# Layer 0's running maximum, over pairs of chunks as b + relu(a - b), with the row maximum inside one VectorE instruction

## The chip, the cores and the metric

One core of one Trainium2 chip runs the whole program. The metric is device microseconds from start to end; lower is better. The engines are TensorE (PE, with weight loads listed as PEld), VectorE (DVE), ScalarE (ACT), GpSimd (POOL) and SyncE (SP), which issues the DMAs.

## The reference

Two perceiver layers on x (1 x 128 x 256). The change touches the first block of layer 0, a cross attention of 128 queries over 12544 keys, 16 heads of 16 channels:

```python
q = (query @ Wq + bq).reshape(B, Nq, H, D).transpose(0, 2, 1, 3)
k = (key_value @ Wk + bk).reshape(B, Nkv, H, D).transpose(0, 2, 1, 3)
v = (key_value @ Wv + bv).reshape(B, Nkv, H, D).transpose(0, 2, 1, 3)
attn = jnp.einsum('bhqd,bhkd->bhqk', q, k) * scale
attn = jax.nn.softmax(attn, axis=-1)
x = jnp.einsum('bhqk,bhkd->bqhd', attn, v).reshape(B, Nq, Cq)
```

The rest (a gated linear attention, two feed-forward blocks, a masked cross attention with 64-channel heads, a self attention with distance bias) is the same in both kernels.

## The kernel before

The softmax of layer 0's cross attention takes two passes over the keys. A first pass (the maximum pass) finds each query's and head's largest score in a coarse product. A second pass (the sum pass) computes the exponentials and weighs the values. Both go by chunks of 896 keys (`CH`), 14 of them (`NCH`); a chunk's columns are two halves of 448 (`NB`).

In the maximum pass SP loads a chunk's context into `raw`. ACT rounds it into `ct` (`split_max0`, two casts). PE projects it to keys in four blocks (`project_max0`, two matmuls each, PSUM banks 4 and 5) and ACT adds the bias and stores each block in `kn` (`key_block_max0`). For each of 16 heads PE multiplies the head's queries with the two halves of the keys into a pair of PSUM banks (`heads_max0`). Three pairs of banks take turns (`HEAD_BANKS`), so a head's matmuls wait until the head three places before it has been read. Even heads are read by DVE, which reduces the 896 scores to one (`reduce_head`, line 813). Odd heads are read by ACT, which casts them to bf16 into one of two `stage` buffers (line 555), and DVE takes an elementwise maximum of that into `acc`, which holds one row of 896 running maxima for each odd head (`accumulate_head`, line 819). After the last chunk DVE halves `acc` three times and reduces it (lines 878 and 880). `merge_max0` (line 823) folds the even heads' maxima into `mx`.

No order is written down beyond program order on each engine; semaphores do the rest. PE's queue has, for each chunk, heads 0 to 2, a block of the next chunk's projection, heads 3 to 5, a block, and so on. ACT has besides, in the first chunks, seven counts of the mask (`mask_sum`), and ahead of chunk 12 two sums over the feed-forward weights (line 580), which SP loads once the seventh count is done. The last chunk's maximum pass is interleaved with the first chunk's exact projection (`project0`, five matmuls of 448 columns) and values (`values0`, five of 256), whose results are read by ACT and DVE (`key_block_hi`, `key_block_lo`, the copies on line 870). At the start POOL fills `acc` (line 390) and part of `ks` (line 398), and takes the power that the first layer norm needs between those two (line 385).

## Time and profile before

| | |
|---|---|
| time, median of 3 runs | 1162.57 us (1161.85 to 1162.88) |
| profiled execution, its own time | 1163.62 us |
| its span, first to last instruction | 1161.8 us |
| maximum pass, first head matmul to last merge | 28.1 to 243.7 us of the span |
| ACT's first read of a head | 30.4 us of the span |
| PE busy in the span | 958.8 us (83%) |
| DVE busy in the span | 645.5 us (56%) |
| ACT busy in the span | 539.8 us (46%) |

The span is shorter than the execution's own time by what lies around the first and last instruction. Busy shares over the whole span average stages with different limits; the maximum pass is some 215 us of them. "Granted clock" is the share of full speed at which TensorE was allowed to run.

### The profile page before, as it was taken

To read this page: it belongs to the slowest core of one execution; us is meant where nothing else is said; L and a number is where in the kernel's file an instruction comes from. 1 tells how busy PE (TensorE), PEld (TensorE's weight loads), DVE (VectorE), ACT (ScalarE), POOL (GpSimd) and SP (SyncE) were. 2 spreads that over 40 slices of the span, in tenths; PEclk is the share of its full clock that TensorE was granted. 3 is DMA by queue.
4 is the path that set the end of the run, shared out by engine and by line. 5 is a ranking of instruction groups with operands and counts; after the bars stand their busy time and mean duration, and the time that the engine had idled before them with its cause. 6 is when DMAs were issued, how large, how long until landed. Compare 5 with 4: busy or idle time off the path is not lost.

```text
span 1161.8 us, 21208 instructions
## 1 busy us (share of the span) xinstructions
PE 958.8 (83%) x7648; PEld 702.1 (60%) x7651; DVE 645.5 (56%) x936; ACT 539.8 (46%) x626; POOL 176.2 (15%) x93
## 2 busy tenths in 40 slices
PE   3877888749899999999969578886999979998514
PEld 2544555537677777777747365555777767776403
DVE  4777999862111222222250237994779757777592
ACT  2787888626666666666646313002333323332011
POOL 4000000141111111111193031242004030000000
PEclk9978999878999999999999689998999989999665
DMA  7213121154556555566614332211001000000000
GB/s 209 82 30 120 48 70 57 33 126 95 129 128 152 131 126 126 134 146 145 144 32 97 109 101 56 64 36 32 1 5 33 1 6 1 1 1 1 1 0 5
DMA packets 37319, 81.73 MB, mean 70 GB/s; under 512 B 9553, under 2 KB 17426, under 8 KB 37138
## 3 DMA queue, kind: packets, MB, share of 16 engines
q1 hardware_dynamic: 37266, 81.01, 28.1%
q8 instruction: 35, 0.57, 0.2%
q14 instruction: 18, 0.15, 0.0%
HBM read 41.54 MB, written 0.13 MB: 36 GB/s over the span
## 4 chain that ended last, share of the span: by engine, by line
PE 46%; issue 19%; DVE 11%; SPq 9%; DMA 7%; ACT 6%; POOL 1%; DVEq 1%; ACTq 0%; POOLq 0%
PE ps L1498 10%; SPq L310 8%; DMA ks<-khl 6%; PE ps L1508 6%; PE ps L1291 5%; PE ps L1519 5%; PE ps L1303 4%; PE ps L1273 4%; PE ps L1245 4%; PE ps L1500 2%; DVE cm L813 2%; ACT pr L555 1%; DVE pr L819 1%; DMA raw<-in_ctxT 1%; PE ps L1282 1%
## 5 line engine op out<-in xcount | busy, mean ns | idle before, releaser
L617 ACT ACTIVATE pr<-ps 128x1024 f32<-128x1024 f32 x196 | 200.0, 1026 | 131.7 <-DVEq L966 127.9
L1291 PE MATMUL ps<-qs,ks 128*128 128x256 f32 x784 | 147.0, 310 | 21.8 <-DMA ks<-khl 13.9
L1245 PE MATMUL ps<-ks 128*128 128x448 f32 x448 | 134.5, 422 | 33.7 <-ACT pr L555 14.3
L1291 PEld LDWEIGHTS ps<-qs,ks 128*128 128x128 f32 x784 | 106.8, 192 | 64.2 <-issue 33.0
L695 ACT ACTIVATE pr<-ps 128x1024 f32<-128x1024 f32 x56 | 57.5, 1027 | 184.7 <-DVE ps L1096 184.7
L1498 PE MATMUL ps<-ks,ct 128*128 128x512 f32 x448 | 128.3, 408 | 7.2 <-issue 4.6
L813 DVE TENSOR_REDUCE cm<-ps 128x1 f32<-128x896 f32 x112 | 120.5, 1084 | 16.9 <-PE ps L1245 16.0
L1245 PEld LDWEIGHTS ps<-ks 128*128 128x128 f32 x448 | 80.7, 206 | 76.8 <-DVE cm L813 28.0
L1303 PE MATMUL ps<-pr,v 128*17 128x128 f32 x3136 | 124.6, 277 | 0.2 <-ACT pr L617 0.2
L847 DVE SCALAR_TENSOR_TENSOR khl<-ps,bk,khl 128x448 fp32r<-128x448 f32 x56 | 38.2, 682 | 151.0 <-ACT khl L592 151.0
L1096 DVE TENSOR_SCALAR ps<-ps 128x1024 f32<-128x1024 f32 x56 | 68.9, 1231 | 76.5 <-PE ps L1500 76.5
L405 POOL TENSOR_TENSOR ct<-raw,ct 128x896 fp32r<-128x896 f32 x14 | 30.6, 2188 | 501.6 <-ACT ct L537 501.6
L910 DVE COPY v<-ps 128x256 f32<-128x256 f32 x91 | 38.6, 424 | 115.1 <-PE ps L1282 115.1
L1498 PEld LDWEIGHTS ps<-ks,ct 128*128 128x128 f32 x448 | 81.2, 190 | 32.1 <-issue 16.6
L1303 PEld LDWEIGHTS ps<-pr,v 128*17 128x17 f32 x3136 | 69.2, 97 | 36.3 <-issue 15.8
L1282 PE MATMUL ps<-wv,ct 128*128 128x256 f32 x490 | 75.1, 283 | 3.2 <-DVE v L870 2.2
L1082 DVE TENSOR_TENSOR nm<-nm,pr 128x1024 f32<-128x1024 f32 x56 | 73.3, 1308 | 2.1
L1273 PE MATMUL ps<-ct,wk 128*128 128x448 f32 x280 | 69.9, 381 | 2.2 <-POOL ct L408 1.6
L1062 DVE CUSTOM_DVE_ANT_0 pr<-ps,khl 128x896 f32<-128x896 f32 x64 | 67.4, 1086 | 4.5 <-issue 4.2
L1078 DVE TENSOR_TENSOR pr<-pr,wraw 128x1024 f32<-128x1024 f32 x56 | 69.1, 1235 | 0.0
L1282 PEld LDWEIGHTS ps<-wv,ct 128*128 128x128 f32 x490 | 65.4, 190 | 5.4 <-DVE v L870 4.3
L1508 PE MATMUL ps<-ks,ct 128*128 128x512 f32 x280 | 68.6, 391 | 0.0
(259 smaller groups left out, 1325.6 us busy)
## 6 DMA issues: line engine op xcount, KB each, us to landing
ks<-khl SPq DMA_DIRECT2D x168, 224.0 KB, 4.8
raw<-in_ctxT SPq DMA_DIRECT2D x36, 448.0 KB, 3.7
raw<-in_ctxT SPq DMA_DIRECT2D x54, 224.0 KB, 4.2
ffw<-in_mask_q SPq DMA_DIRECT2D x1, 1568.0 KB, 10.0
ffw<-in_W1T SPq DMA_DIRECT2D x1, 1024.0 KB, 4.9
ffw<-in_W2T SPq DMA_DIRECT2D x1, 1024.0 KB, 7.2
pr<-in_Wq SPq DMA_DIRECT2D x1, 1024.0 KB, 5.1
pr<-in_Wkt SPq DMA_DIRECT2D x1, 1024.0 KB, 7.4
```

What stands on the lines that cost most here:

```text
L310: sp.dma_start(ks_v[32 * slot:32 * slot + 32, b, g::4, :].bitcast(F32), khl[32 * g:32 * g + 32, part, :, :].bitcast(F32)).then_inc(S[f"e0_ ...
L617: nc.scalar.activation(pr[:, (HALVES * b + u) % 4, :], bank(2 * (u % 2), 2), ACT.Exp).then_inc(S["e0_exp"], 1)
L813: V.tensor_reduce(cm_e[:, h // 2:h // 2 + 1, b], ps[:, bank:bank + 2, 0:NB], AX_XY, ALU.max).then_inc(S["m0_red"], 1)
L1078: V.tensor_tensor(sl, sl, mk[:, b, u // 2, :].unsqueeze(1).to_broadcast([P, 8, T]), ALU.mult).then_inc(S["e1_masked"], 1)
L1082: V.tensor_tensor(acc, acc, pr[:, (HALVES * b + u) % 4, :], ALU.add).then_inc(S["e1_sum"], 1)
L1245: last = mm(ps[:, bank + n, 0:NB], qn[:, h, :], kn[:, b, t, n * NB:(n + 1) * NB], start=True, stop=True)
L1273: last = mm(dst, wk0[:, w, t * P:(t + 1) * P], ct[:, b, xx, n * NB:(n + 1) * NB], start=(j == 0), stop=(j == 4))
L1282: last = mm(ps[:, bank, 0:C], ct[:, b, xx, t * P:(t + 1) * P], wv0[:, w, :], start=(j == 0), stop=(j == 4))
L1291: last = mm(ps[:, 2 * z + k // 2, (k % 2) * 256:(k % 2) * 256 + 256], ks_v[:, b, gg, t * P:(t + 1) * P], qs[:, gg * 256:gg * 256 + 256], s ...
L1303: last = mm(ps[32 * j:32 * j + 17, 4, (h // 4) * T:(h // 4 + 1) * T], v17_v[:, b, t, h, :], pr[:, (HALVES * b + u) % 4, k * T:(k + 1) * T] ...
L1498: mm(ps[:, 2 * z + j, :], xx[:, t * P:(t + 1) * P], asp[:, w, cols], start=(i == 0), stop=False)
L1508: last = mm(ps[:, 6 + j, :], ct[:, b, xx, t * P:(t + 1) * P], wv1[:, w, 512 * j:512 * j + 512], start=(i == 0), stop=(i == 4))
```

## The change

Chunks are taken in pairs, a the second and b the first, so there are seven pairs (`NSUP`). The product with a head's queries is linear in the keys, and max(a, b) = b + relu(a - b). ACT stores the keys of b (`base_keys`, both halves at once); DVE subtracts them from the projected keys of a (`key_differences`). For each head PE makes two products, called units: unit 2h with the key differences, unit 2h + 1 with b's keys. Units take the three pairs of banks in turn. ACT reads unit 2h through relu into one of four fp32 `stage` slots (`above_base`); DVE adds unit 2h + 1 from PSUM to that slot and takes the row maximum in the same instruction (`head_max`, behind a memset of one element). `merge_max0` comes once a pair. `acc` and its halving are gone, and with them POOL's first fill; POOL's second fill is shorter, and the rest of it comes at the start of the last pair. In the first pair ACT's queue has the casts of chunks 2 and 3 ahead of the first relu. A block of the projection is now four matmuls. The second of two `kn` buffers lies in the part of `ks` that is free in this pass.

The diff, without most of the lines that it takes out (they stand in the kernel above):

```diff
+UNITS = 2 * H
+SLOTS = 4
+
+
+def unit_bank(u):
+
+    return HEAD_BANKS[u % 3]
+
+
+def last_user(u):
+
+    if u >= 3:
+        return 0, u - 3
+    return -1, max(v for v in range(UNITS) if v % 3 == u % 3)
...
-        kn = ks[:, k0_at + HQ:].rearrange("p (b t n) -> p b t n", b=2, t=2)
+        kn = [ks[:, k0_at + HQ:].rearrange("p (e t n) -> p e t n", e=2, t=2),
+              ks[:, 0:4 * CH].rearrange("p (e t n) -> p e t n", e=2, t=2)]
...
-        acc = pr_flat[:, 0:4 * CH].bitcast(BF16).rearrange("p (j n) -> p j n", j=8)
-        stage = [oacc_flat[:, 0:CH // 2].bitcast(BF16),
-                 pr_flat[:, 4 * CH:4 * CH + CH // 2].bitcast(BF16)]
+        stage = pr_flat[:, 0:SLOTS * CH].rearrange("p (i k n) -> p i k n", i=SLOTS, k=2)
...
             load_max0(3, False)
-            load_max0(4, False)
-            load_max0(5, False)
+            with sp.Fori(4, 11) as c:
+                load_max0(c, False)
             sp.wait_ge(S["mask_sum"], NSUP)
             load(ffw1, a["W1T"].rearrange("(k p) n -> p k n", k=2), "ld_ffw")
             load(ffw2, a["W2T"].rearrange("(k p) n -> p k n", k=8), "ld_ffw")
 
-            with sp.Fori(6, NCH) as c:
+            with sp.Fori(11, NCH) as c:
                 load_max0(c, False)
...
 
 
-            pool.wait_ge(S["acc_init"], 1)
             pool.wait_ge(S["power"], 1)
-            nc.gpsimd.memset(ks[96:P, 0:k0_at - 8 * T].bitcast(F32), 1.0).then_inc(S["ks_ones"], 1)
+            nc.gpsimd.memset(ks[96:P, 4 * CH:k0_at - 8 * T].bitcast(F32), 1.0).then_inc(S["ks_ones"], 1)
...
             split_lo0(0, 0)
+            pool.wait_ge(S["e0_lo"], 2)
+            pool.wait_ge(S["m0_head"], UNITS * NSUP)
+            nc.gpsimd.memset(ks[96:P, 0:4 * CH].bitcast(F32), 1.0).then_inc(S["ks_ones"], 1)
+            pool.wait_ge(S["ks_ones"], 2)
             split_lo0(1, 1)
...
-                act.wait_ge(S["m0_proj"], 4 * c + 4)
+                act.wait_ge(S["m0_proj"], 2 * c + 2)
...
-            def key_block_max0(c, b, i):
-                t, n = i // 2, i % 2
-                if i == 0:
-                    act.wait_ge(S["m0_head"], H * c + H)
-                act.wait_ge(S["m0_proj"], 4 * c + i + 9)
-                nc.scalar.activation(kn[:, b, t, n * NB:(n + 1) * NB], ps[:, 4 + i % 2, 0:NB], ACT.Identity,
-                                     bias=bk0[:, t:t + 1]).then_inc(S["m0_keys"], 1)
+            def base_keys(s, t):
+
+                if t == 0:
+                    act.wait_ge(S["m0_head"], UNITS * s)
+                act.wait_ge(S["m0_proj"], 4 * s + t + 5)
+                nc.scalar.activation(kn[s % 2][:, 0, t, :].rearrange("p (k n) -> p k n", k=2), ps[:, 4:6, 0:NB],
+                                     ACT.Identity, bias=bk0[:, t:t + 1]).then_inc(S["m0_keys"], 1)
...
+            def above_base(s, h):
+
+                at = unit_bank(2 * h)
+                act.wait_ge(S["m0_head"], UNITS * s + 2 * h + 1 + UNITS)
+                act.wait_ge(S["m0_red"], H * s + h - SLOTS + 1 + H)
+                nc.scalar.activation(stage[:, h % SLOTS], ps[:, at:at + 2, 0:NB], ACT.Relu
+                                     ).then_inc(S["m0_staged"], 1)
+
+            split_max0(0, 0)
+            for t in range(2):
+                base_keys(0, t)
+            split_max0(1, 1)
+            split_max0(2, 0)
+            split_max0(3, 1)
+            for s in range(NSUP - 1):
+                for h in range(H):
+                    above_base(s, h)
+                    if h in (3, 6):
+                        base_keys(s + 1, (3, 6).index(h))
+                    if h == 8:
+                        if s < NSUP - 2:
+                            split_max0(2 * s + 4, 0)
+                        else:
+                            act.wait_ge(S["m0_proj"], 4 * (NSUP - 1) + 6)
                             split_hi0(0, 0)
...
+                    if h == 14 and s < NSUP - 2:
+                        split_max0(2 * s + 5, 1)
+                    if h in (10, 12) and 2 * s + (h - 10) // 2 < NSUP:
+                        mask_sum(2 * s + (h - 10) // 2)
+                if s == 4:
+                    act.wait_ge(S["ld_ffw"], 32)
+                    act.wait_ge(S["mask_sum"], NSUP)
+                    for k in range(2):
+                        nc.scalar.activation(scrap, ffw[:, 2048 * k:2048 * k + 2048], ACT.Abs,
+                                             accum_out=wsum[:, k:k + 1]).then_inc(S["wsum"], 1)
+                        act.wait_ge(S["wsum"], k + 1)
...
-            for j in range(8):
-                act.wait_ge(S["m0_head"], H * (NCH - 1) + 2 * j + 34)
-                act.wait_ge(S["m0_acc"], 8 * (NCH - 1) + j + 1)
-                nc.scalar.copy(stage[j % 2].rearrange("p (k n) -> p k n", k=2), ps[:, 2:4, 0:NB]
-                               ).then_inc(S["m0_staged"], 1)
-                if j < 4:
-                    key_block_hi(0, j, 22 + j + 1, None)
-            act.wait_ge(S["m0_proj"], 4 * NCH + 8)
+            for h in range(H):
+                above_base(NSUP - 1, h)
+                if h in (2, 4, 6, 8):
+                    i = h // 2 - 1
+                    key_block_hi(0, i, 22 + i + 1, None, at=4)
...
+
+            def key_differences(s, t, buf):
+
+                dve.wait_ge(S["m0_head"], UNITS * s)
+                dve.wait_ge(S["m0_keys"], 2 * s + t + 1)
+                dve.wait_ge(S["m0_proj"], 4 * s + t + 7)
+                V.scalar_tensor_tensor(kn[buf][:, 1, t, :].rearrange("p (k n) -> p k n", k=2), ps[:, 4:6, 0:NB],
+                                       bk0[:, t:t + 1],
+                                       kn[buf][:, 0, t, :].rearrange("p (k n) -> p k n", k=2).bitcast(F32),
+                                       ALU.add, ALU.subtract).then_inc(S["m0_diff"], 1)
+
+            def head_max(s, h):
+
+                at = unit_bank(2 * h + 1)
+                dve.wait_ge(S["m0_head"], UNITS * s + 2 * h + 2 + UNITS)
+                dve.wait_ge(S["m0_staged"], H * s + h + 1 + H)
+                V.memset(pause2[:, h % 2:h % 2 + 1], 0.0)
+                nc.vector.tensor_tensor_reduce(
+                    out=stage[:, h % SLOTS], in0=ps[:, at:at + 2, 0:NB], in1=stage[:, h % SLOTS],
+                    scale=1.0, scalar=-3.0e38, op0=ALU.add, op1=ALU.max,
+                    accum_out=cm[:, h:h + 1]).then_inc(S["m0_red"], 1)
+
+            def merge_max0(s):
+
+                dve.wait_ge(S["m0_red"], H * s + 2 * H)
+                V.tensor_tensor(mx[:, :], mx[:, :], cm[:, :], ALU.max).then_inc(S["m0_merge"], 1)
+
+            def pair_max0(s, buf):
+                dve.wait_ge(S["m0_merge"], s + 1)
+                for h in range(H):
+                    head_max(s, h)
+                    if h in (9, 12):
+                        key_differences(s + 1, (9, 12).index(h), 1 - buf)
+                merge_max0(s)
+
+            for t in range(2):
+                key_differences(0, t, 0)
+            pair_max0(0, 0)
+            with dve.Fori(1, NSUP - 2, 2) as s:
+                for e in range(2):
+                    pair_max0(s + e, 1 - e)
+            pair_max0(NSUP - 2, 1)
+
...
-            dve.wait_ge(S["m0_merge"], NCH)
...
-                if h % 2 == 0:
-                    reduce_head(NCH - 1, 1, h, 0)
-                else:
-                    accumulate_head(NCH - 1, h // 2)
-                if h == 2:
-                    merge_max0(NCH - 2, 0)
+                head_max(NSUP - 1, h)
                 if h in (2, 4, 6, 8):
-                    key_block_lo(0, h // 2 - 1)
+                    key_block_lo(0, h // 2 - 1, at=4)
...
-            merge_max0(NCH - 1, 1)
-            dve.wait_ge(S["m0_merge"], NCH + 2)
-            dve.wait_ge(S["m0_acc"], 8 * NCH + 2)
-            n = CH // 2
-            while n >= CH // 8:
-                link(V.tensor_tensor(acc[:, :, 0:n], acc[:, :, 0:n], acc[:, :, n:2 * n], ALU.max))
-                n //= 2
-            link(V.tensor_reduce(mx_e[:, :, 1], acc[:, :, 0:CH // 8], AX_X, ALU.max))
+            merge_max0(NSUP - 1)
+            dve.wait_ge(S["m0_merge"], NSUP + 1)
...
-            def project_max0(c, b, blocks=range(4)):
-                if 0 in blocks:
-                    pe.wait_ge(S["m0_split"], c + 1)
-                for i in blocks:
-                    t, n = i // 2, i % 2
-                    pe.wait_ge(S["m0_keys"], 4 * c + i + 3)
-                    dst = ps[:, 4 + i % 2, 0:NB]
-                    mm(dst, wk0[:, W_AH, t * P:(t + 1) * P], ct[:, b, X_AH, n * NB:(n + 1) * NB],
+            def project_max0(s, e, t):
+
+                if t == 0:
+                    pe.wait_ge(S["m0_split"], 2 * s + e + 1)
+                if (e, t) in ((0, 0), (1, 1)):
+                    pe.wait_ge(S["m0_diff"], 2 * s + t + 2)
+                else:
+                    pe.wait_ge(S["m0_keys"], 2 * s + e + 1)
+                for n in range(2):
+                    dst = ps[:, 4 + n, 0:NB]
+                    mm(dst, wk0[:, W_AH, t * P:(t + 1) * P], ct[:, e, X_AH, n * NB:(n + 1) * NB],
                        start=True, stop=False)
-                    mm(dst, wk0[0:64, W_BH, t * P:(t + 1) * P], ct[0:64, b, X_B, n * NB:(n + 1) * NB],
-                       start=False, stop=True).then_inc(S["m0_proj"], 1)
-
-            def heads_max0(c, b, heads, last_chunk=False):
+                    last = mm(dst, wk0[0:64, W_BH, t * P:(t + 1) * P], ct[0:64, e, X_B, n * NB:(n + 1) * NB],
+                              start=False, stop=True)
+                last.then_inc(S["m0_proj"], 1)
+
+            def heads_max0(s, buf, heads):
                 for h in heads:
                     t = h // 8
                     if h % 8 == 0:
-                        pe.wait_ge(S["m0_keys"], 4 * c + 2 * t + 6)
-
-
-
-                    bank = head_bank(b, h)
-                    back, user = last_user(b, h)
-                    if last_chunk:
-                        bank = 2 * (h % 2)
-                        back, user = (0, h - 2) if h > 1 else (-1, {0: H - 1, 1: H - 3}[h])
-                    pe.wait_ge(S["m0_staged" if user % 2 else "m0_red"],
-                               8 * (c + back) + user // 2 + 1 + 8)
-                    for n in range(2):
-                        last = mm(ps[:, bank + n, 0:NB], qn[:, h, :],
-                                  kn[:, b, t, n * NB:(n + 1) * NB], start=True, stop=True)
-                    last.then_inc(S["m0_head"], 1)
+                        pe.wait_ge(S["m0_keys"], 2 * s + t + 1)
+                        pe.wait_ge(S["m0_diff"], 2 * s + t + 3)
+                    for u, e in ((2 * h, 1), (2 * h + 1, 0)):
+                        back, user = last_user(u)
+                        pe.wait_ge(S["m0_red" if user % 2 else "m0_staged"],
+                                   H * (s + back) + user // 2 + 1 + H)
+                        for n in range(2):
+                            last = mm(ps[:, unit_bank(u) + n, 0:NB], qn[:, h, :],
+                                      kn[buf][:, e, t, n * NB:(n + 1) * NB], start=True, stop=True)
+                        last.then_inc(S["m0_head"], 1)
 
             pe.wait_ge(S["w0_hi"], 1)
             pe.wait_ge(S["qn"], 1)
-            project_max0(0, 0)
-
-            def chunk_max0(c, b):
+            for e in range(2):
+                for t in range(2):
+                    project_max0(0, e, t)
+
+            def pair_max0(s, buf):
 
                 for i in range(4):
-                    heads_max0(c, b, range(3 * i, 3 * i + 3))
...
-            with pe.Fori(0, NCH - 2, 2) as c:
-                for b in range(2):
-                    chunk_max0(c + b, b)
-            chunk_max0(NCH - 2, 0)
-
-            def project0(c, b, i):
+                    heads_max0(s, buf, range(3 * i, 3 * i + 3))
+                    project_max0(s + 1, i // 2, i % 2)
+                heads_max0(s, buf, range(12, H))
+
+            pair_max0(0, 0)
+            with pe.Fori(1, NSUP - 2, 2) as s:
+                for e in range(2):
```

In PE's queue inside a chunk, before: the last head unit of a group of three, the projection block, and the next unit. A row with `m0_red` waits for DVE, one with `m0_staged` for ACT.

```order
L1245 MATMUL ps<-ks 128x448 [waits m0_red]
L1245 MATMUL ps<-ks 128x448
L1222 REGISTER_ALU
L1224 MATMUL ps<-ct,wk 128x448 [waits m0_keys]
L1226 MATMUL ps<-ct,wk 128x448
L1245 MATMUL ps<-ks 128x448 [waits m0_staged]
L1245 MATMUL ps<-ks 128x448
```

The same place in the changed kernel, in its first pair (line 1234 is a unit's matmul, 1217 and 1219 are the projection's):

```order
L1234 MATMUL ps<-ks 128x448 [waits m0_red]
L1234 MATMUL ps<-ks 128x448
L1234 MATMUL ps<-ks 128x448 [waits m0_staged]
L1234 MATMUL ps<-ks 128x448
L1217 MATMUL ps<-ct,wk 128x448 [waits m0_keys]
L1219 MATMUL ps<-ct,wk 128x448
L1217 MATMUL ps<-ct,wk 128x448
L1219 MATMUL ps<-ct,wk 128x448
L1234 MATMUL ps<-ks 128x448 [waits m0_red]
```

The block has become twice as long, it stands behind three heads of two units each, and the unit behind it waits for DVE.

ACT's queue ahead of its first read of a head, before (522 and 523 are a chunk's casts, 530 a key block):

```order
L522 CAST ct<-raw 128x896 [waits m0_proj,m0_raw]
L523 CAST ct<-raw 64x896
L530 ACTIVATE ks<-ps,bk 128x448 [waits m0_proj,m0_head]
L530 ACTIVATE ks<-ps,bk 128x448 [waits m0_proj] x3
L522 CAST ct<-raw 128x896 [waits m0_proj,m0_raw]
L523 CAST ct<-raw 64x896
L555 CAST oacc<-ps 128x896 [waits m0_acc,m0_head]
```

And in the changed kernel (520 and 521 are the casts, 528 the keys of b, 552 the relu):

```order
L520 CAST ct<-raw 128x896 [waits m0_proj,m0_raw]
L521 CAST ct<-raw 64x896
L528 ACTIVATE ks<-ps,bk 128x896 [waits m0_proj,m0_head]
L528 ACTIVATE ks<-ps,bk 128x896 [waits m0_proj]
L520 CAST ct<-raw 128x896 [waits m0_proj,m0_raw]
L521 CAST ct<-raw 64x896
L520 CAST ct<-raw 128x896 [waits m0_proj,m0_raw]
L521 CAST ct<-raw 64x896
L520 CAST ct<-raw 128x896 [waits m0_proj,m0_raw]
L521 CAST ct<-raw 64x896
L552 ACTIVATE pr<-ps 128x896 [waits m0_red,m0_head] x4
```

Four chunks are cast ahead of the first relu, where two were cast ahead of the first read.

## Rows read from the trace of the kernel before

**Rows 1.** Busy time of each engine in one steady chunk, granted clock behind POOL.

```profile
163.07:175.67 12.60, 11.11 (x42) 6.56 (x40) 12.50 (x19) 10.61 (x15) 0.00 (x0) 1.00 0.18 55
```

**Rows 2.** Timeline of a steady stretch, PE's weight loads: start, length, both in us.

```profile
117.18 0.19 PEld L1224 LDWEIGHTS ps<-ct,wk 128*128 128x128 f32 x1
...
118.07 0.71 PEld L1245 LDWEIGHTS ps<-ks 128*128 128x128 f32 x4 [0.21 <-issue]
```

**Rows 3.** Timeline, from a unit's first weight load to its reader on ACT.

```profile
212.20 0.70 PEld L1245 LDWEIGHTS ps<-ks 128*128 128x128 f32 x4 [0.21 <-issue]
...
212.91 0.91 ACT L555 CAST oacc<-ps 128x896 bf16<-128x896 f32 x1 [0.15 <-PE ps L1245]
```

**Rows 4.** Timeline, ACT at work without a wait.

```profile
118.77 0.96 ACT L522 CAST ct<-raw 128x896 fp32r<-128x896 f32 x1
...
120.45 0.90 ACT L555 CAST pr<-ps 128x896 bf16<-128x896 f32 x1
121.25 0.64 ACT L530 ACTIVATE ks<-ps,bk 128x448 fp32r<-128x448 f32 x1
...
121.78 0.90 ACT L555 CAST oacc<-ps 128x896 bf16<-128x896 f32 x1
```

**Rows 5.** Timeline of layer 1's maximum pass: an add with row maximum, and PE behind it.

```profile
713.17 1.09 DVE L1062 CUSTOM_DVE_ANT_0 pr<-ps,khl 128x896 f32<-128x896 f32 x1
...
714.32 0.19 PEld L1476 LDWEIGHTS ps<-ct,ks 128*128 128x128 f32 x1 [0.32 <-DVE cm L1062]
```

**Rows 6.** Groups by line: the fused bias and subtraction, columns count, busy, mean ns.

```profile
L847 DVE SCALAR_TENSOR_TENSOR khl<-ps,bk,khl 128x448 fp32r<-128x448 f32 x56 | 38.2, 682 | 151.0 <-ACT khl L592 151.0
```

**Rows 7.** Timeline of the start: POOL, DVE, ACT, PE and SP's queue (SPq).

```profile
1.04 6.07 POOL L390 MEMSET pr<- 128x7168 bf16 x1
...
3.52 0.15 DVE L755 TENSOR_SCALAR rstd<-mv 128x1 f32<-128x1 f32 x1
...
7.74 6.73 DVE L758 TENSOR_SCALAR xn<-x,mv,rstd 128x256 f32<-128x256 f32 x1 [4.07 <-POOL rstd L385]
7.83 6.49 POOL L398 MEMSET ks<- 32x7680 f32 x1
...
9.29 0.40 ACT L514 CAST wv<-wraw 128x256 fp32r<-128x256 f32 x1
...
15.37 0.37 ACT L505 COPY xnT<-ps 128x256 f32<-128x256 f32 x1 [5.67 <-PE ps L1196]
...
19.51 0.98 SPq L240 DMA_DIRECT2D raw<-in_ctxT  x2
...
22.76 0.71 PE L1224 MATMUL ps<-ct,wk 128*128 128x448 f32 x1 [3.15 <-issue]
...
24.07 0.74 PE L1224 MATMUL ps<-ct,wk 128*128 128x448 f32 x1
...
24.73 7.81 SPq L281 DMA_DIRECT2D qs<-ks  x12
...
37.41 0.94 ACT L522 CAST ct<-raw 128x896 fp32r<-128x896 f32 x1 [1.89 <-DMA raw<-in_ctxT]
```

**Rows 8.** Timeline around the weights' loads and the sums over them.

```profile
94.27 0.39 SPq L240 DMA_DIRECT2D ffw<-in_W1T  x1
...
104.49 0.94 ACT L522 CAST ct<-raw 128x896 fp32r<-128x896 f32 x1 [3.38 <-DMA raw<-in_ctxT]
...
204.10 1.91 ACT L580 ACTIVATE v<-ffw 128x2048 bf16<-128x2048 f32 x1
...
206.13 0.91 ACT L555 CAST oacc<-ps 128x896 bf16<-128x896 f32 x1
```

**Rows 9.** Timeline of the last chunk and what follows it.

```profile
237.17 0.65 PEld L1282 LDWEIGHTS ps<-wv,ct 128*128 128x128 f32 x5 [1.06 <-DVE v L870]
...
243.73 7.31 DVE L878 TENSOR_TENSOR pr<-pr 128x3584 bf16<-128x3584 bf16 x3
...
252.20 0.17 DVE L891 TENSOR_SCALAR mx<-mx 128x16 f32<-128x16 f32 x1
```

122 lines of the change are left out of this document (26 added, 96 removed).

## The prediction

> **What bounds the kernel now.** I read the page first (PE 83% busy, no engine full), then the maximum pass stretch by stretch, then single hand-overs in the timeline. In a steady chunk of 12.60 us DVE is busy for 12.50, PE for 11.11 and ACT for 10.61, at granted clock 1.00 [rows 1]. The reader is to see that DVE alone sets the pace: eight reductions, eight adds of staged maxima and a merge. Two chunks cost 25.2 us. After the last merge three halvings and a reduction of the running maxima hold everything up, from 243.73 to the next step at 252.20 [rows 9]. The pass starts late because DVE's layer-norm step takes 6.73 us while POOL fills `ks` for 6.49, and POOL's power ahead of it stood behind another fill of 6.07 [rows 7].
>
> **The work of a pair, by counts.** ACT: 16 relus of 896 columns 0.80 apart (120.45 to 121.25), four casts at 1.68 for a chunk's two (118.77 to 120.45), two key stores that take 0.53 at 448 columns and by the columns about 0.9 at 896 [rows 4]: 18.0 us. DVE: 16 add-and-maximum instructions at most 1.15 apart [rows 5], two key differences (0.68 at 448 columns [rows 6], so about 1.1), a merge: 21 us. PE: a projection part of two matmuls takes 0.89 (117.18 to 118.07), so a block of four 1.78, four blocks 7.1; a unit takes about 0.4 (four loads in 0.71, matmuls behind them) [rows 2], 32 units 12.8: 20 us. By counts a pair would fall from 25.2 to 21.
>
> **What the order makes of it.** Unit 2h goes into the banks that unit 2h - 3 used, which DVE read for head h - 2. So there is a loop: DVE done with head h - 2, PE makes unit 2h, ACT takes its relu, DVE adds head h. Before, ACT's read gave its banks back without DVE. The links: from a unit's first load to its reader 0.71 (212.20 to 212.91) [rows 3]; the relu 0.91, as the cast of the same columns, and 0.04 to hand over; from the start of DVE's instruction to PE's next load 1.15 (713.17 to 714.32; layer 1's pass has the same memset and instruction) [rows 5]. Together 2.81 for two heads, 22.5 a pair if nothing stands in the way.
>
> But each engine takes its queue in order, and the loop has no room to catch up. I walked one pair through at full clock: L is the first load of unit 2h, A the relu's start, D DVE's. L(h) is the latest of D(h-2) + 1.15 and PE being free; unit 2h + 1 goes 0.4 later, but not before A(h-1) is over; A(h) is L + 0.71 or ACT free; D(h) is A + 0.95 or DVE free. A block of 1.78 stands on PE behind h = 2, 5, 8, 11; key stores on ACT behind 3 and 6, casts behind 8 and 14; differences on DVE behind 9 and 12.
>
> | h | L | A | D |
> |---|---|---|---|
> | 0 | 0 | 0.71 | 1.66 |
> | 1 | 1.40 | 2.11 | 3.06 |
> | 2 | 2.81 | 3.52 | 4.46 |
> | 3 | 5.40 | 6.11 | 7.06 |
> | 4 | 6.20 | 7.76 | 8.71 |
> | 6 | 10.90 | 11.61 | 12.56 |
> | 9 | 16.40 | 17.11 | 18.06 |
> | 10 | 17.20 | 17.91 | 20.14 |
> | 12 | 22.10 | 22.81 | 23.76 |
> | 15 | 26.99 | 28.10 | 29.05 |
>
> Each block takes PE for 1.78 where the loop leaves it 0.6 a head, and delays L by 1.2 to 1.5 (5.40 where 4.21 was due); the parity of the delayed head changes, so nothing is won back. The next pair's first two units wait for ACT's and DVE's last head (`last_user` wraps to units 30 and 31): its second unit goes at 30.2, and its h = 3 at 34.64. So a pair takes 34.64 - 5.40 = **29.2 us**, 4.0 more than now. Bounds: 22.5 if blocks cost nothing, 29.2 plus some for the clock (below).
>
> **Start.** The fill of `acc` is gone, so the power can follow DVE's step of 3.52 at once and the layer norm is released near 4.3. POOL's remaining fill is 4096 of 7680 columns, 6.49 x 0.53 = 3.46, and DVE gets through with it near 7.9 instead of 14.5. ACT, however, casts weights until 9.69 (9.29 + 0.40), so its copy of 15.37 comes at 9.7: 5.7 us earlier [rows 7]. PE's first projection moves from 22.76 to 17.1.
>
> That is lost again. Chunk 1 is loaded from 19.51, which SP's queue of small loads sets, and with the 4.9 us that chunk 2 needed (32.54, the end of the 12 DMAs, to 37.41) it lands at 24.4 or a little later. ACT casts it (1.68), until 26.5. SP's 12 DMAs for the queries now run from 20.5 to 28.3 (7.81), chunk 2's load follows and lands at 33.2, its cast ends at 35.0, chunk 3's load needs that cast, lands at 39.8, and is cast until 41.5. Only then comes the first relu, where ACT's first read was at 30.4 (table of the profile before); the loads' times are from [rows 7]. In the walk A(0) is 0.71, so the pair starts at 40.8. PE has waited and runs at half clock at first (two matmuls 1.31 apart, 22.76 to 24.07 [rows 7], a block 2.62): h = 3 stands at 47.6 instead of 46.2, 1.4 more. Start of the pair: 42.2.
>
> Here the Trainium skill's page "SBUF — State Buffer", section "Who interferes with whom", is weighed: a DVE instruction in a two-port mode and a GpSimd one block each other for a whole instruction, whoever issues first. In this trace DVE was released at 7.74, before POOL's 7.83, and still took 6.73 [rows 7]. By the row the layer norm ends near 7.9, by the rule with DVE first some 3 us sooner. The sum is the same, since ACT's weight casts end at 9.69 either way.
>
> **The rest of the pass.** Six pairs: 6 x 29.2 = 175.2. Seven mask counts, two a pair: each holds ACT some 1.8 (2.03 for 2048 columns [rows 8], here 1792), most of it in ACT's gaps; in the walk a pair with two ends 0.6 later: 2.1. Weights: SP loads them after the seventh count and chunk 11 behind them; from 94.27 to 104.49 that took 10.2 [rows 8]. The count now ends at 20.6 of pair 3, chunk 11 lands at 30.9, and its cast is due at 26.4: 4.5. The sums over the weights hold ACT 4.1 (2 x 2.03) where 0.9 of it was idle: 3.1. After these two holds PE is at half clock for some us: 1 each, 2 (0 to 4). Last pair: same walk with five-matmul projections behind h = 1, 3, 5, 7 and values behind 8 to 14. It goes like the others until 13.0; then the first values wait for DVE's last key block (16.4), and each further head costs PE two units, five value matmuls (0.65 [rows 9]) and a wait for DVE's copy of the values two before, 1.2 to 2.4. D(15) starts at 30.0 and the merge ends at 31.3.
>
> Sum: 42.2 + 175.2 + 2.1 + 4.5 + 3.1 + 2 + 31.3 = 260.4, where the next step now starts at 252.20 [rows 9], and there is no halving. 8.2 us later. Behind it nothing is new: keys are stacked by DMA meanwhile, POOL's casts and fill lie beside the small steps, and its fill of 3584 columns (3.0) lies at the start of the last pair, where POOL has no reader waiting. The profiled execution took 1163.62, so 1171.8; that is 1.05 above the median, so **1171 us**.
>
> **Rivals.**
> *The pace follows the counts* (faster). If PE's blocks did not hold the loop, a pair would take 21 to 22.5: 6.4 pairs x 7 = 45 less than my sum, about 1127. For it: DVE's pace now is by counts. Against: now ACT's read frees its banks at once, so queues run ahead; in layer 1's pass, with a loop of the same kind, DVE stands behind PE. 0.08.
> *The blocks hold it half as much* (faster): a pair at 26.2, 19 less, 1152. A pair of 27.9 decides the sign (8.2 / 6.4 = 1.3 below mine). For it: my 1.78 comes from two parts with 64-row matmuls between, and two in a row may take less. Against: the 0.89 that I doubled already holds both changes, to 64 rows and back [rows 2]. 0.15.
> *The clock falls in the pass* (slower still). At half clock a unit takes 0.65 and a block 2.62, PE needs 32 us a pair; half the time so would add 1.5 to 4 a pair, some 19: 1190. For it: PE waits in every head. Against: a waiting PE shows clock 1.00 in the steady chunks, and at half clock it would have no gaps left. 0.12.
> The Trainium skill's page "TensorE: Matmul & The Clock Gate", section "A second HAM failure mode: psum-queue depth-cycling", says that cycling through PSUM banks idles PE briefly and often enough for its clock to swing. By that rule this last rival holds; the steady chunks cycle through three pairs of banks at clock 1.00 [rows 1] and don't show it.
> My own case, slower by the loop, 1163 to 1179: 0.65.
>
> **How the numbers follow.** A measurement of this kernel tells 0.2% (2.3 us) from no change. Faster: 0.08 + most of the half-hold rival, 0.21. Same: the lower edge of my case and a bit of that rival, 0.09. Slower: 0.70. The range 1148 to 1188 holds my case, most of the half-hold rival and half of the clock's, 0.82; my case's own range is 1163 to 1179.
>
> **What would show it.** A pair of some 29.2 between two merges; relus that wait for PE and PE's loads that wait for DVE in the loop's order, with DVE busy below 80%; first relu near 41.5 behind two DMA waits of ACT; the small steps after the last merge near 260. Wrong if pairs are at 22 to 26, if the clock in the pass is below 0.9, or if the first relu is before 38.

## The result

The changed kernel takes **1179.76 us** (median of four, 1179.06 to 1181.1) where the kernel before took 1162.72 in the same comparison (1161.85 to 1164.24). The two medians divide to 1.0147; the ratio on record is 1.0154, 95% interval 1.0139 to 1.0169. Slower was forecast, by 8.4; measured are 17.0. The profiled execution has a span of 1179.2 against 1161.8. One execution of e4 below (1212.41 at a granted clock of 0.80, where its others had 0.914 to 0.918) fell in a slow state and is left out of every figure.

From the page of the changed kernel, the groups by line (busy us, mean ns, then idle time ahead of them and what ended most of it):

```profile
L1234 PE MATMUL ps<-ks 128*128 128x448 f32 x448 | 142.9, 449 | 39.5 <-ACT pr L552 22.1
L819 DVE CUSTOM_DVE_ANT_0 pr<-ps,pr 128x896 f32<-128x896 f32 x112 | 121.1, 1088 | 43.9 <-PE ps L1234 32.3
L1234 PEld LDWEIGHTS ps<-ks 128*128 128x128 f32 x448 | 89.7, 223 | 85.2 <-ACT pr L552 34.7
L552 ACT ACTIVATE pr<-ps 128x896 f32<-128x896 f32 x112 | 101.2, 917 | 77.1 <-PE ps L1234 75.8
```

Over the pass no engine is the bottleneck, all wait in a ring: ScalarE's relu for TensorE (75.8), VectorE's add for TensorE (32.3), TensorE for ScalarE and VectorE. In a steady chunk of before VectorE had nothing to wait for [rows 1].

The stretches between merges of the changed kernel, from 74.50 on (merges at 74.50, 107.28, 137.41, 172.02, 201.69, 237.20, 270.21); columns: length, busy time of PE, PEld, DVE, ACT and POOL with counts, granted clock, DMA share, GB/s:

```profile
74.50:107.28 32.78, 29.29 (x80) 17.75 (x80) 19.79 (x52) 22.20 (x26) 0.00 (x0) 0.76 0.13 41
107.28:137.41 30.13, 25.65 (x80) 14.97 (x80) 19.70 (x52) 22.31 (x26) 0.00 (x0) 0.90 0.16 47
137.41:172.02 34.61, 25.25 (x80) 15.16 (x80) 19.63 (x51) 20.89 (x24) 0.00 (x0) 0.89 0.29 100
172.02:201.69 29.67, 24.49 (x80) 14.75 (x80) 19.55 (x51) 20.36 (x23) 0.00 (x0) 0.94 0.17 50
201.69:237.20 35.51, 28.61 (x80) 17.16 (x80) 19.83 (x52) 20.27 (x25) 5.60 (x3) 0.76 0.15 47
237.20:270.21 33.01, 26.48 (x117) 21.36 (x117) 23.02 (x62) 18.05 (x22) 1.69 (x1) 0.90 0.40 84
```

VectorE works 19.6 of some 30 a pair, 65%. Below, these are the first to the sixth stretch; the first pair ends at 74.50, so the first stretch is the second pair. The third holds the wait for chunk 11, the fifth (201.69) the sums over the weights. The eye should go to the clock: 0.76 twice, and 0.87 over 42.20 to 270.20, where a steady chunk of before stood at 1.00 [rows 1] and its whole pass (28.10 to 243.73) at 0.93.

The start, in ScalarE's timeline (start, length, in brackets the idle time ahead and what ended it):

```profile
27.61 0.94 ACT L520 CAST ct<-raw 128x896 fp32r<-128x896 f32 x1 [3.40 <-DMA raw<-in_ctxT]
28.45 0.93 ACT L521 CAST ct<-raw 64x896 fp32r<-64x896 f32 x1
34.12 0.94 ACT L520 CAST ct<-raw 128x896 fp32r<-128x896 f32 x1 [4.74 <-DMA raw<-in_ctxT]
34.97 0.93 ACT L521 CAST ct<-raw 64x896 fp32r<-64x896 f32 x1
40.50 0.94 ACT L520 CAST ct<-raw 128x896 fp32r<-128x896 f32 x1 [4.60 <-DMA raw<-in_ctxT]
41.34 0.93 ACT L521 CAST ct<-raw 64x896 fp32r<-64x896 f32 x1
42.18 1.71 ACT L552 ACTIVATE pr<-ps 128x896 f32<-128x896 f32 x2
```

Two casts that wait for their loads stand ahead of the first relu at 42.18, as forecast (41.5). TensorE's first projection went from 22.76 [rows 7] to 16.54 (forecast 17.1), which is worth nothing.

And what follows the last merge, where before the next step came at 252.20 behind the halvings [rows 9]:

```profile
270.21 0.17 DVE L827 TENSOR_TENSOR mx<-mx,cm 128x16 f32<-128x16 f32 x1
270.41 0.17 DVE L881 TENSOR_SCALAR mx<-mx 128x16 f32<-128x16 f32 x1
270.48 2.07 POOL L400 TENSOR_TENSOR ct<-raw,ct 128x896 fp32r<-128x896 f32 x1 [31.60 <-ACT ct L535]
270.62 1.96 DVE L874 TENSOR_SCALAR mx<-mx 128x16 f32<-128x16 f32 x1
272.62 0.18 DVE L875 CAST mhi<-mx 128x16 fp32r<-128x16 f32 x1
272.63 2.09 POOL L403 TENSOR_TENSOR ct<-raw,ct 64x896 fp32r<-64x896 f32 x1
272.83 1.93 DVE L877 COPY ml<-mhi 128x16 f32<-128x16 f32 x1
274.79 0.18 DVE L878 TENSOR_TENSOR ml<-mx,mhi 128x16 f32<-128x16 f32 x1
275.09 5.07 PE L1316 MATMUL ps<-con,ml 128*32 128x128 f32 x32 [6.96 <-DVEq L879]
```

Two of VectorE's steps on 16 columns take 1.96 and 1.93 where their neighbours take 0.17: each begins just behind one of POOL's subtractions and ends with it. So the lateness grows from 18.2 (270.41 against 252.20) to 21.8 at TensorE's row step (275.09 against 253.34), falls to 19.6 at the first exponential (286.52 against 266.92; the row step itself is shorter, 5.07 against 6.27, and the clock up to the first exponential is 0.87 against 0.63), stays there through layer 0's sum pass and layer 1's maximum, is 19.0 at the last exponential (1087.92 against 1068.95), and 17.4 at the end.

### The profile page after: what moved, and what is told of

It reads as the page before. It is cut to its first block, busy times and chain, and to the rows that moved or that the text cites. A ratio compares the mean times of both kernels' runs of the same rounds, so it can differ in the third digit from the quotient of the medians.

```text
span 1179.2 us, 21097 instructions
## 1 busy us (share of the span) xinstructions
PE 972.6 (82%) x7651; PEld 707.5 (60%) x7651; DVE 596.5 (51%) x1051; ACT 524.1 (44%) x584; POOL 168.0 (14%) x93
## 4 chain that ended last, share of the span: by engine, by line
PE 49%; issue 17%; SPq 10%; DVE 8%; DMA 8%; ACT 7%; DVEq 1%; POOL 0%; ACTq 0%; POOLq 0%
PE ps L1491 10%; SPq L307 8%; PE ps L1234 7%; DMA ks<-khl 6%; PE ps L1501 5%; PE ps L1283 5%; PE ps L1512 4%; PE ps L1295 4%; PE ps L1265 3%; ACT pr L552 3%; PE ps L1493 2%; DMA raw<-in_ctxT 2%; SPq L237 2%; PE ps L1219 1%; PE ps L1217 1%
## 5 line engine op out<-in xcount | busy, mean ns | idle before, releaser
L1234 PE MATMUL ps<-ks 128*128 128x448 f32 x448 | 142.9, 449 | 39.5 <-ACT pr L552 22.1
L819 DVE CUSTOM_DVE_ANT_0 pr<-ps,pr 128x896 f32<-128x896 f32 x112 | 121.1, 1088 | 43.9 <-PE ps L1234 32.3
L1234 PEld LDWEIGHTS ps<-ks 128*128 128x128 f32 x448 | 89.7, 223 | 85.2 <-ACT pr L552 34.7
L552 ACT ACTIVATE pr<-ps 128x896 f32<-128x896 f32 x112 | 101.2, 917 | 77.1 <-PE ps L1234 75.8
L1068 DVE TENSOR_TENSOR pr<-pr,wraw 128x1024 f32<-128x1024 f32 x56 | 69.1, 1234 | 0.0
```

The costliest lines, as they stand in the source:

```text
L552: nc.scalar.activation(stage[:, h % SLOTS], ps[:, at:at + 2, 0:NB], ACT.Relu).then_inc(S["m0_staged"], 1)
L819: nc.vector.tensor_tensor_reduce(out=stage[:, h % SLOTS], in0=ps[:, at:at + 2, 0:NB], in1=stage[:, h % SLOTS], scale=1.0, scalar=-3.0e38, ...
L1068: V.tensor_tensor(sl, sl, mk[:, b, u // 2, :].unsqueeze(1).to_broadcast([P, 8, T]), ALU.mult).then_inc(S["e1_masked"], 1)
L1234: last = mm(ps[:, unit_bank(u) + n, 0:NB], qn[:, h, :], kn[buf][:, e, t, n * NB:(n + 1) * NB], start=True, stop=True)
```

## The experiments

Thirteen kernels, four of them (e5, e6, e12, e13) run once. Medians stand against the runs of the kernel before that shared their chip (1161.4 to 1162.2). Where a stretch between two merges is read, it is of the one profiled execution, which for e1, e2, e7, e8 and e9 was the fastest of its kernel and for the changed kernel the slowest (1181.1).

### The order of units (e1)

A is the unit of a head that ScalarE reads, B its base unit. `pos_a` gives 0, then 2h - 1, `pos_b` 2h + 2 (the last 31), and `step_units(h)` the units A(h+1) and B(h); the waits on banks follow the new sequence.

```diff
-                    for u, e in ((2 * h, 1), (2 * h + 1, 0)):
+                for step in heads:
+                    for u, h, e in step_units(step):
...
-                at = unit_bank(2 * h)
+                at = unit_bank(pos_a(h))
...
-                at = unit_bank(2 * h + 1)
+                at = unit_bank(pos_b(h))
```

Expected: 

> Same instructions as the changed kernel; only the order of TensorE's 32 units of a pair is another: the unit that ScalarE's relu of head h+1 reads is issued ahead of the base unit of head h (A0, A1, B0, A2, B1, ..., A15, B14, B15). Loop theory (the pair's pace is the serial loop VectorE -> unit 0.71 -> relu 0.95 -> VectorE 1.15, 2.81 per two heads, plus the holds by the projection blocks): with the new order a base unit's bank is freed by the relu, and the loop closes over three heads instead of two, 0.71 + 0.95 + 0.71 + 1.15 = 3.5 to 3.6 per three heads, 1.19 a head instead of 1.41; 16 of them 19.1, the blocks and ScalarE's key stores and casts on top, pair 24 to 26 instead of 29.2 to 30. Kernel 1145 (1138 to 1155). Count or clock theory (the pass is slow because of how much the engines do, or because TensorE runs at half clock in stretches): nothing is done less, so 1178 to 1181.

Measured: 1156.93 (1152.95 to 1162.43, ten runs), ratio to the kernel before 0.9967 [0.9949, 0.9984]: a little faster than before, 23 below the changed kernel, but above the 1138 to 1155 expected. Its first two stretches:

```profile
69.37:96.58 27.21, 22.56 (x80) 13.41 (x80) 19.83 (x52) 22.24 (x27) 0.00 (x0) 1.00 0.18 54
96.58:123.81 27.23, 22.64 (x80) 13.44 (x80) 19.82 (x52) 22.36 (x27) 0.00 (x0) 1.00 0.17 51
```

The same 80 matmuls and the same work of VectorE and ScalarE in 27.2 instead of 30.1 and 32.8. Counts can't explain that. But 24 to 26 was expected: ScalarE is now busy 22.2 of 27.2, so its key stores, casts and sums show, which a loop alone leaves out (e8, with the sums elsewhere, comes to 26.2). The clock is 1.00 here without any work added, so part of the gain goes with the clock. How much is the order's alone, two stretches below tell, both without mask sums: 28.83 at 0.99 in the old order (e7), 26.17 at 1.00 in the new one (e8), 2.7 less.

### Blocks in halves (e2)

`HALVES_AT` is (1, 2, 4, 5, 7, 8, 10, 11), and the first key difference moves from behind head 9 to behind head 8.

```diff
-                for i in range(4):
-                    heads_max0(s, buf, range(3 * i, 3 * i + 3))
-                    project_max0(s + 1, i // 2, i % 2)
-                heads_max0(s, buf, range(12, H))
+                for h in range(H):
+                    heads_max0(s, buf, [h])
+                    if h in HALVES_AT:
+                        i = HALVES_AT.index(h)
+                        project_max0(s + 1, i // 4, i // 2 % 2, (i % 2,))
```

Expected: 

> Each projection block of four matmuls (1.78 us on TensorE) is issued as two halves of two matmuls, one head apart (behind heads 1 and 2, 4 and 5, 7 and 8, 10 and 11), and the first key difference of the next pair stands behind head 8 instead of 9. Loop theory (a block holds the loop for what it is longer than the slack of the unit that waits behind it): a half of 0.9 us fits mostly into TensorE's own idle of a head, pair 26.5 to 27.5 instead of about 29.8, kernel 1165 (1158 to 1172). If a block cost the loop its whole length wherever it stands (no slack to hide in), 1178 to 1181; if switches between 128-row and 64-row matmuls are what costs, the same, since their number is the same.

Measured: 1172.72 (1170.35 to 1174.34), 1.0095 [1.0079, 1.011]. 7 us less, half of what was expected. The fourth stretch, against 29.67 at 0.94 in the changed kernel:

```profile
165.09:193.57 28.48, 23.80 (x80) 14.44 (x80) 19.63 (x51) 20.42 (x23) 0.00 (x0) 0.95 0.17 50
```

1.2 less, where about 3 was expected. If each of the four blocks held the loop for 1.7, and halves hid in TensorE's idle time, far more would have come back. That made the parts of the predicted pair doubtful, though not their sum.

### Relu on half the columns (e5)

```diff
-                nc.scalar.activation(stage[:, h % SLOTS], ps[:, at:at + 2, 0:NB], ACT.Relu
+                nc.scalar.activation(stage[:, h % SLOTS, 0, :], ps[:, at, 0:NB], ACT.Relu
...
-                    out=stage[:, h % SLOTS], in0=ps[:, at:at + 2, 0:NB], in1=stage[:, h % SLOTS],
+                    out=nm[:, (h % 2) * CH:(h % 2) * CH + CH].rearrange("p (k n) -> p k n", k=2), in0=ps[:, at:at + 2, 0:NB],
+                    in1=stage[:, h % SLOTS, 0:1, :].to_broadcast([P, 2, NB]),
```

Expected: 

> Left out: the relu of half the columns. ScalarE's relu reads one bank (448 columns instead of 896) and VectorE adds that half to both of its banks; TensorE's work, VectorE's work and every wait are unchanged, and ScalarE has far less to do. Loop theory (the relu's 0.95 stands in the serial loop once in two heads of VectorE -> unit -> relu -> VectorE): relu 0.53 instead of 0.92, 0.4 less per two heads, 3.1 a pair, 22 over seven pairs; kernel 1158 (1153 to 1163). Count theory (VectorE's 21 or TensorE's 20 a pair, or TensorE's half clock, set the pace, ScalarE is only waited for in passing): 1178 to 1181.

Measured: 1160.02 in its one run. The fourth stretch, and its relu (544 ns instead of 917):

```profile
157.38:184.06 26.68, 22.94 (x80) 14.49 (x80) 19.60 (x52) 14.69 (x23) 0.00 (x0) 0.96 0.18 53
L552 ACT ACTIVATE pr<-ps 128x448 f32<-128x448 f32 x16 | 8.7, 544 | 13.2 <-PE ps L1235 13.2
```

2.99 less than 29.67, where eight times 0.37 is 2.98. ScalarE had been idle a third of the pair, and still each microsecond of its relu counted, once in two heads. That is the signature of a serial loop. The agreement to a hundredth is in part luck, since the clock is 0.96 here and 0.94 there; in e7 below 0.04 of clock went with 0.5 us a pair.

### What the pair is made of (e6, e12, e13)

e6 leaves out the projections of the pass behind the first pair's:

```diff
+                if not in_full:
+                    pe.sem_inc(S["m0_proj"], 1)
+                    return
```

Expected: 

> Left out: the projections of the key chunks 2 to 13 in the maximum pass (the first pair's keys are used again); the waits ahead of a block stay, its four matmuls go, in six pairs of four blocks. Everything else is as in the changed kernel. Loop theory with blocks that hold the loop (29.2 a pair of which 22.5 is the bare loop and the rest the holds by blocks, 1.7 each): pair 22.5 to 24, six of them 36 to 42 less, kernel 1141 (1136 to 1146). If the two-matmul halves of the other experiment gained so little (1.1 a pair) because the blocks are mostly hidden already and the bare loop is the longer term: pair 27 or more, kernel 1163 or more. That the clock falls further with less work on TensorE would show as 0.5 to 0.8 in a pair's row and a pair between the two.

Measured: 1163.82 in its one run, a miss: 1141 was expected. Its fourth stretch:

```profile
158.84:185.74 26.90, 19.21 (x64) 11.27 (x64) 19.56 (x52) 20.43 (x23) 0.00 (x0) 0.94 0.18 54
```

26.90 without a single block, where the bare loop was to be 22.5. Two kernels took that apart. e13 keeps the blocks and leaves out ScalarE's key stores and casts and VectorE's differences, with the sums ahead of the pass; e12 leaves the blocks out too, by the edit of e6. The form of the edit, at the key stores and the differences (the casts likewise):

```diff
-                        base_keys(s + 1, (3, 6).index(h))
+                        act.wait_ge(S["m0_proj"], 4 * (s + 1) + (3, 6).index(h) + 5)
+                        act.sem_inc(S["m0_keys"], 1)
...
-                        key_differences(s + 1, (9, 12).index(h), 1 - buf)
+                        dve.wait_ge(S["m0_keys"], 2 * s + 2 + (9, 12).index(h) + 1)
+                        dve.wait_ge(S["m0_proj"], 4 * s + 4 + (9, 12).index(h) + 7)
+                        dve.sem_inc(S["m0_diff"], 1)
```

Expected: 

> Left out in the six first pairs of the changed kernel: the projection blocks, ScalarE's key stores and casts, VectorE's key differences (their waits and counts stay; the first pair's keys are used throughout), and the seven mask sums stand ahead of the first relu, which therefore starts 13 later. What is left is the units, the relus and the adds. The loop as predicted: 2.81 per two heads, so a pair of 22.5 to 22.7 between two merges at full clock (the third pair longer by its load wait). If the bare loop is itself longer than its links (the blocks' kernel showed pairs of 26.9 without any block): 25 or more. Read by pairs; the whole time, 1151, has no other meaning.

Expected: 

> As the kernel above it in this call, with the four projection blocks of a pair left in (they project chunks that are in place). As predicted, a block holds the loop for 1.2 to 1.5 of its 1.78: pair 27.3 to 28.5. With the 4.4 that ScalarE's and VectorE's other work adds to a pair without blocks (26.9), the two would sum to 32 or more, and pairs with both are 28.8 at full clock: so either a block alone holds less than predicted (pair of 25 or less), or the two holds fall into each other's shadow (pair of 27.3 to 28.5 here).

Measured: 1151.39 and 1166.65, one run each. A stretch of each (e12's third, e13's second), e12 first:

```profile
125.40:148.35 22.95, 17.99 (x64) 10.22 (x64) 17.72 (x49) 14.68 (x17) 0.00 (x0) 1.00 0.45 151
```

```profile
110.13:136.92 26.79, 22.75 (x80) 13.65 (x80) 17.36 (x49) 14.31 (x17) 0.00 (x0) 1.00 0.17 53
```

And the bare loop of e12 in VectorE's timeline:

```profile
113.03 1.09 DVE L824 CUSTOM_DVE_ANT_0 pr<-ps,pr 128x896 f32<-128x896 f32 x1
...
114.72 1.09 DVE L824 CUSTOM_DVE_ANT_0 pr<-ps,pr 128x896 f32<-128x896 f32 x1 [0.60 <-PE ps L1244]
...
115.84 1.09 DVE L824 CUSTOM_DVE_ANT_0 pr<-ps,pr 128x896 f32<-128x896 f32 x1
...
117.54 1.08 DVE L824 CUSTOM_DVE_ANT_0 pr<-ps,pr 128x896 f32<-128x896 f32 x1 [0.60 <-PE ps L1244]
```

115.84 - 113.03 = 2.81, 117.54 - 114.72 = 2.82: two heads, to the hundredth the sum of three hand-overs that were read elsewhere in the kernel before. A bare pair is 22.95. Blocks alone add 3.85 (0.96 each, not 1.2 to 1.5; the pair of 26.8 is just below the 27.3 to 28.5 expected), the other engines' work alone 3.95 (e6, but at clock 0.94, so some of it is the clock's), both together 5.9 (28.83 in e7 below, clock 0.99). The two holds lie partly in each other's shadow: at like clock, taking away the blocks gives back 2.8 (29.67 and 26.90, both at 0.94), taking away the other work 2.0 (28.83 at 0.99 and 26.79 at 1.00), and not 4.

### The start (e3)

```diff
-            split_max0(2, 0)
-            split_max0(3, 1)
             for s in range(NSUP - 1):
                 for h in range(H):
                     above_base(s, h)
+                    if s == 0 and h in (0, 2):
+                        split_max0(2 + (h == 2), int(h == 2))
```

Expected: 

> ScalarE's casts of chunks 2 and 3, which stand ahead of the first relu and wait for their loads (first relu at 42.18, while TensorE's first unit was ready at 36.2), are moved into the first pair, behind the relus of heads 0 and 2. Theory of the start (the casts and their loads hold the first relu, not TensorE or VectorE): first relu at 36.5 to 37.5, the last merge and everything behind it 4 to 5 earlier, kernel 1175 (1172 to 1177). Rival: the load of chunk 3 (it lands at 40.5 only) then holds TensorE's first block or ScalarE in the pair instead and takes back all but 1: 1178 to 1180.

Measured: 1177.26 (1176.35 to 1177.7), 1.0127 [1.0112, 1.0143], 2.5 less than the changed kernel, between what the theory (1172 to 1177) and its rival (1178 to 1180) gave. Its first relu and first stretch:

```profile
35.68 0.92 ACT L552 ACTIVATE pr<-ps 128x896 f32<-128x896 f32 x1 [8.00 <-PE ps L1234]
71.89:101.14 29.25, 24.83 (x80) 14.20 (x80) 19.84 (x51) 21.77 (x26) 0.00 (x0) 0.93 0.15 45
```

The relu is 6.5 earlier, as the theory of the start had it, and the first merge 2.6 (71.89 against 74.50): chunk 3 is still waited for, inside the pair. That stretch is the telling one. Instruction for instruction it is the changed kernel's of 32.78 at 0.76, and it takes 29.25 at 0.93 (in e4 below 30.92 at 0.89). Each is cut in two where VectorE's add for head 6 starts, the changed kernel first:

```profile
74.50:89.55 15.05, 14.84 (x36) 9.76 (x36) 6.79 (x20) 7.16 (x9) 0.00 (x0) 0.59 0.10 35
89.55:107.28 17.73, 14.45 (x44) 7.99 (x44) 13.00 (x33) 15.05 (x18) 0.00 (x0) 0.90 0.17 45
```

```profile
71.89:83.39 11.50, 10.11 (x36) 6.20 (x36) 6.79 (x19) 6.71 (x9) 0.00 (x0) 1.00 0.12 45
83.39:101.14 17.75, 14.72 (x44) 8.00 (x44) 13.05 (x32) 15.06 (x18) 0.00 (x0) 0.88 0.17 46
```

The second parts agree to 0.02. All of the 3.5 us lies in the first parts, the same 36 matmuls at clock 0.59 and at 1.00; from 74.50 to 86.50 the changed kernel was at the lower of the two levels, 0.50. So 3.5 us of a pair are the clock's alone. What made it fall here and not there these rows don't tell: TensorE's last instructions ahead of it, with their gaps of 0.60, 0.53, 0.61 and 0.92, are the same in both to 0.01.

### GpSimd behind VectorE's small steps (e4)

```diff
             pool.wait_ge(S["ks_ones"], 2)
+            pool.wait_ge(S["m0_ml"], 1)
             split_lo0(1, 1)
             pool.wait_ge(S["e0_lo"], 3)
-            pool.wait_ge(S["m0_ml"], 1)
```

Expected: 

> GpSimd's cast of chunk 1's low parts (two subtractions, 2.07 and 2.09 us) waits until VectorE's small steps behind the last merge are done (m0_ml), instead of running beside them. Port theory (VectorE's steps on 128x16 that took 1.96 and 1.93 instead of 0.17 were held by GpSimd's two subtractions, which since the change fall onto them): both steps take 0.2, TensorE's row step starts at about 271.5 instead of 275.09, kernel 1176.3 (1175 to 1178), and the subtractions end before TensorE's first use of chunk 1. Rival (they are slow for another reason, as the end of the loop or code loading, or GpSimd's later end is waited for instead): 1179 to 1181.

Measured: 1178.58 (1173.81 to 1179.33, four runs), 1.013 [1.0109, 1.0151], 1.2 below the changed kernel where 3.5 was expected, and the two intervals overlap. The timeline behind its last merge at 267.59:

```profile
268.00 0.17 DVE L874 TENSOR_SCALAR mx<-mx 128x16 f32<-128x16 f32 x1
268.21 0.18 DVE L875 CAST mhi<-mx 128x16 fp32r<-128x16 f32 x1
268.42 0.18 DVE L877 COPY ml<-mhi 128x16 f32<-128x16 f32 x1
...
268.93 5.05 PE L1316 MATMUL ps<-con,ml 128*32 128x128 f32 x32 [3.42 <-DVEq L879]
269.01 2.07 POOL L400 TENSOR_TENSOR ct<-raw,ct 128x896 fp32r<-128x896 f32 x1 [31.71 <-DVEq L879]
```

From merge to row step 1.34 instead of 4.88: 3.5, as expected, and it is GpSimd that held the two steps. But in the profiled execution the sum pass behind it took 378.5 from first to last exponential where it was 375.2; it lost that in its first chunks, and its first 47 us ran at a granted clock of 0.93 (0.96 in the changed kernel). So in this kernel the gain hardly reached the end. e11 below tries it again.

### More work for TensorE, to keep its clock (e9)

```diff
-                        for n in range(2):
+                        for n in (0, 1) if e else (0, 0, 1):
```

Expected: 

> The changed kernel with one matmul more in each base unit: its first one is issued twice, with the same result. That gives TensorE 0.2 more to do per head in its own idle time, behind the difference unit and ahead of a result that VectorE needs only after the relu. Clock theory (TensorE falls to half clock in the pass, 0.76 to 0.94 granted, because it waits a third of the time; pairs of the same instructions were 28.8 at 0.99, 29.3 at 0.95, 30.1 at 0.90 and 32.8 at 0.76): the clock rises to 0.95 or more, pairs 28.8 to 29.5 and no pair of 32.8, kernel 1172 to 1176. If the granted clock has nothing to do with that, or more work on TensorE lengthens the loop: pairs of 30 to 31.5, 1181 to 1190.

Measured: 1181.55 (1176.2 to 1182.19), 1.0168 [1.0151, 1.0186], the time that the rival gave. The first stretch of the profiled execution, which was the fastest (granted clock over the whole run 0.929, in the others 0.921 to 0.924):

```profile
73.99:104.05 30.06, 26.34 (x96) 16.50 (x96) 19.80 (x51) 22.37 (x27) 0.00 (x0) 1.00 0.15 45
```

Both theories have half of it. In that execution the clock is at least that of the changed kernel in each of the six stretches (1.00, 1.00, 0.93, 0.95, 0.81, 1.00 against 0.76, 0.90, 0.89, 0.94, 0.76, 0.90), with nothing changed but a matmul in each gap; and the added matmuls hold the loop, so a pair is 30.1 at full clock instead of 28.8. No gain.

### Sums and weights out of the pass, and the combinations (e7, e8, e10, e11)

e7 is e3 with this edit, and the pairs behind the first without their mask sums; e8 is e7 with the order of e1; e10 is e8 with the halves of e2; e11 is e10 with the edit of e4.

```diff
             for t in range(2):
                 base_keys(0, t)
+                mask_sum(t)
             split_max0(1, 1)
+            for i in (2, 3, 4):
+                mask_sum(i)
...
-            with sp.Fori(4, 11) as c:
+            for c in (4, 5):
                 load_max0(c, False)
             sp.wait_ge(S["mask_sum"], NSUP)
```

Expected: 

> The kernel with the casts of chunks 2 and 3 in the first pair (the one before in this study, 1177.3), and on top five of the seven mask sums (1.9 us each) in ScalarE's idle time while it waits for the first loads, the other two in the first pair, and the loads of W1T and W2T behind those of chunk 5 instead of ahead of that of chunk 11. Loop theory (ScalarE is idle a quarter of a pair and a sum there costs next to nothing; the load wait of the third pair is one of 4.5): pairs 1, 2 and 4 unchanged at 29.3 to 29.8, the third 29.7 instead of 34.2, kernel 1172.5 (1170 to 1175). Theory that ScalarE's sums hold the loop for their whole length like a block: 1.9 per sum more in the pairs 1 to 3 (five sums), kernel 1163 to 1167.

Measured: 1169.8 (1168.89 to 1172.87), 1.0072 [1.0047, 1.0097], 7.5 below e3. Its second and third stretch:

```profile
99.50:128.33 28.83, 23.28 (x80) 13.56 (x80) 19.56 (x51) 19.06 (x23) 0.00 (x0) 0.99 0.17 48
128.33:157.63 29.30, 24.16 (x80) 14.41 (x80) 19.55 (x51) 19.33 (x23) 0.00 (x0) 0.95 0.16 47
```

The third is the one that was 34.16 in e3: the load wait is gone. Mask sums in a pair cost it nothing at about the same clock (29.38 at 0.95 without them, 29.25 at 0.93 with them in e3), but without them the clock stayed nearer to 1 in this one profile (0.95, 0.99, 0.95, 0.99 against 0.93, 0.90, 0.90, 0.94), which may be why the time fell below the 1170 to 1175 expected.

Expected: 

> The order of units of the first experiment (1156.9, pairs of 27.2 at full clock) with the start, the mask sums and the weight loads of the kernel above it in this call. If the pieces add: first relu at 35.7 instead of 40.8 (-5), no load wait in the third pair (-4.3), and ScalarE, which in that order is idle only 4.4 of 27.2 behind TensorE, loses 3.8 of sums in pairs 1 and 2 and half of it shows (-3 to -6): 1144 (1140 to 1148), faster than the kernel before (1162). If only the start and the load wait count: 1148.

Measured: 1150.41 (1145.54 to 1154.22), 0.9907 [0.9876, 0.9939], 2.4 above the upper end of what was expected (1140 to 1148). In its fastest execution, which was profiled: first relu at 36.19, pairs of 26.2 at clock 0.98 to 1.00 and 27.0 at 0.94 to 0.96. The weight sums still cost it 2.4 in their pair (29.46).

Expected: 

> The fastest so far (difference units one head ahead, early start, early mask sums and weight loads: 1150.4) with each projection block in two halves. In the old order the halves gave 1.1 a pair. Here the order leaves TensorE's idle in smaller pieces, and the block's hold is the largest term left (pair 26.2 to 27.0 of which 19.1 is the bare loop): halves 1 to 2 a pair less, kernel 1143 (1138 to 1148). If what is left is ScalarE's 20 a pair with its key stores and casts rather than the blocks: 1149 to 1152.

Measured: 1144.92 (1143.79 to 1146.47), 0.9851 [0.9832, 0.987]. A pair at full clock, 1.0 less than e8's:

```profile
120.39:145.56 25.17, 21.92 (x80) 13.34 (x80) 19.94 (x52) 19.07 (x23) 0.00 (x0) 1.00 0.18 54
```

Expected: 

> The same, and GpSimd's cast of chunk 1's low parts behind VectorE's small steps. Small steps 3.5 shorter as in its own run; there 3.3 of it was given back in the first three chunks of the pass behind, at a granted clock of 0.93 and 0.96 against 0.96 and 1.00. If that was the clock's chance: 3.5 less than the kernel above it in this call. If the later cast itself causes it: the same within 1.

Measured: 1141.75 (1139.81 to 1145.31), 0.9824 [0.9803, 0.9845], 3.2 below e10 where 3.5 was expected, though the ranges of the two overlap. From the last merge to the first exponential 14.99 instead of 18.30, and the sum pass takes 375.4 as in e10 (375.3). So a later cast does not by itself lengthen that pass; what e4 lost there went with its lower clock. This kernel is 1.8% faster than the one before and 3.2% faster than the changed one (1141.75 against 1179.76), with the same arithmetic.

## Why the prediction came out as it did

**What bounded the kernel, and the counts.** Right. Counts are 19.6 to 19.8 for VectorE in a pair; the rival by counts (a pair of 21 to 22.5) is dead: pairs took 29.7 to 32.8 with these counts, and e1 changed no count and took 2.4 to 5.6 us off a pair.

**The loop.** Right in place and size: 2.81 for two heads forecast, 2.81 and 2.82 measured in e12. e5 fits the relu's part, 2.99 a pair for 0.37 a relu, at a clock 0.02 higher.

**The pair of 29.2.** 28.8 at clock 0.99 (e7), 0.4 too long. Its parts were not read rightly. "22.5 if blocks cost nothing" put all of the 6.7 on the blocks; without them a pair is 26.90 (e6), since ScalarE's and VectorE's own work holds the loop too. The walk's rules had that in them: worked again (my estimate, from the prediction's own links) they give some 27.4 with the blocks alone, 26.1 with the other work alone and 22.9 with neither, where 26.8, 26.9 (at clock 0.94) and 22.95 were measured. A block alone costs 0.96, less than the walk's 1.2 to 1.5; on TensorE it takes 1.68 (175.72 to 177.40, first load to the next unit's) and not the 1.78 of twice 0.89. The rival of blocks that hold it half as much (26.2 a pair) did not come, because what blocks don't hold, the other work does. That the pair came out near 29.2 is thus the walk's merit and not that of the sentence on the blocks.

**The start.** Right: 41.5 forecast, 42.18 measured, chunk loads behind each other. VectorE's normalizing step took 3.68 beside GpSimd's fill of 3.51, as the row of before had said. What the forecast called half clock there the recorded clock doesn't show: the first projections' matmuls take 0.74 each where later ones take 0.47, at a granted clock of 1.00 in the rows.

**The step that failed, first part: the clock.** The sum held 2 us for half clock after two holds, and the rival of a falling clock was thought unlikely because the steady chunks of before stood at 1.00. Measured against the walk, the small steps began 10.0 later than forecast (270.41 against 260.4). By merges: the first was due at 42.2 + 29.05 + 1.15 + 0.6 = 73.0 and is at 74.50 (+1.5, of which 0.7 start); the pairs behind it were due at 29.8, 29.8, 35.0, 29.2 and 33.3 and differ by +3.0, +0.3, -0.4, +0.5 and +2.2, the last one (31.3 less the 1.0 by which it starts ahead of the merge) by +2.7. The +3.0 is the pair at 0.76, which e3 ran in 3.5 less at 0.93. The +2.2 is the other at 0.76 and the +2.7 the last, at 0.90; e4, the same kernel in these stretches, ran them 1.3 and 1.4 shorter:

```profile
201.77:235.95 34.18, 26.29 (x80) 15.79 (x80) 19.83 (x52) 20.73 (x25) 5.93 (x3) 0.85 0.16 50
235.95:267.59 31.64, 25.19 (x117) 20.05 (x117) 23.02 (x63) 17.61 (x22) 1.36 (x1) 0.95 0.41 88
```

So 3.0 + 1.3 + 1.4 = 5.7 of the 10.0 go with the clock, on top of the 2 in the sum, by rows of the same instructions. This is the term of the sum that was mis-sized: 2 for half clock, where these rows alone show 3.5 + 1.3 + 1.4 = 6.2 without reaching full clock. That adds up the better row of each stretch; as whole executions, e4's six stretches took 3.4 less than the changed kernel's and e3's 4.3 less (192.28 and 191.45 against 195.71), and none was at 1.00 throughout. The rival "the clock falls in the pass" (0.12, 1190) was thus right in kind, at a third of its size: over the whole pass the granted clock was 0.87. Its own price was off too: it held a unit at 0.65 at half clock, where six units take 5.12 at the lower level (81.17 to 86.29), 0.85 each. And what was said against it, that at half clock TensorE would have no gaps left, came true (14.84 busy of 15.05) and still the clock stayed low for 12 us. The Trainium skill's page "TensorE: Matmul & The Clock Gate", section "A second HAM failure mode: psum-queue depth-cycling", which says of another kernel that short idles from cycling through PSUM banks make the clock swing, was set aside in the prediction by a row at 1.00; the rows of the changed kernel (0.76 to 0.94) and of e9 agree with it, those of e12 (1.00 in three stretches, with pauses in every head) don't, so when it holds stays open.

The row set against the rival was chosen too narrowly. It is one of seven chunks of 12.60 at 1.00, from 116.74 to 204.94 [rows 1]. The four chunks ahead of them in the same trace, with mask counts on ScalarE and the wait for the weights' loads among them, took 14.9 to 17.8 at 0.80 to 0.90, two of them here:

```profile
67.24:84.04 16.80, 13.61 (x41) 8.69 (x42) 12.70 (x18) 13.90 (x18) 0.00 (x0) 0.80 0.14 41
98.95:116.74 17.79, 13.16 (x42) 8.08 (x40) 12.64 (x19) 10.73 (x15) 0.00 (x0) 0.81 0.38 128
```

In those chunks VectorE was busy 12.7 of 16.8 and 12.6 of 17.8 and did not set the pace alone. So the kernel before already showed what its clock does when other work holds the engines unevenly, and the new pass has such work in every pair.

**Second part: "behind it nothing is new".** It named POOL's casts beside the small steps and costed them at nothing. They cost 3.5. In the timeline of the kernel before the two subtractions lie beside the halvings (243.73 to 251.04 [rows 9]):

```profile
244.38 3.30 POOL L405 TENSOR_TENSOR ct<-raw,ct 128x896 fp32r<-128x896 f32 x1 [22.92 <-ACT ct L537]
247.76 2.80 POOL L408 TENSOR_TENSOR ct<-raw,ct 64x896 fp32r<-64x896 f32 x1
```

With the halvings gone they fall on two steps of 0.17, and each is held until the subtraction ends (the subtractions themselves now take 2.07 and 2.09). e4 shows it, 4.88 to 1.34. The Trainium skill's page "SBUF — State Buffer", section "Who interferes with whom", states such a block for a whole instruction; the trace agrees (1.96 and 1.93 instead of 0.17 and 0.18), and the prediction used that very section for the start only.

**Smaller terms.** Weight sums 3.1 and half clock 1 after them were forecast, 35.51 - 29.67 = 5.8 measured (5.4 in e7, 6.7 in e12; but 2.1 in e1, where units one head ahead give the others something to do). Chunk 11's wait: 4.5 forecast, 4.5 measured. The last pair is 31.6 near full clock (e4, e9), where 30.3 from merge to merge was forecast: 1.3 short.

**The end.** 21.8 late at the row step became 19.6 at the first exponential, with the shorter row step and the granted clock at 0.87 there instead of 0.63, and 17.4 at the end. So the 9.2 between the 8.2 forecast and the 17.4 are 10.0 before the small steps and 3.5 in them, less 2.2 up to the first exponential and 2.2 behind it: luck that hid part of the two misses. The last 1.6 are regained behind the last exponential; from there to the end the spans of this study's kernels are 91.2 to 93.0 with the same code, before's 92.9 and the changed one's 91.3, so this may be chance of the executions. It was not settled.

## What to carry to other kernels

Moving work off the busiest engine pays only if the hand-overs don't become a ring that is longer than the work: write down for each buffer who frees it, add the latencies around, and compare with the busiest engine's count. If a ring comes out, issue the producer for the slowest reader one step ahead before taking work away; here that alone turned 1.5% slower into 0.3% faster (2.7 us a pair from the order, the rest from the clock that came with it), and with the start, the sums and the loads moved out of its way into 1.8% faster. When a long instruction disappears, look for what used to run beside it, and price it against what stands there now. And don't take TensorE's clock in the new order from one row of the old one: read the clock of every stretch of the old kernel, and put a price on it from both levels.

## What the hardware showed that was not expected

- The same instructions of a pair took 29.25 at a granted clock of 0.93 and 32.78 at 0.76 (e3 and the changed kernel), and the whole difference lay in the first 15 us, 12 of them at the lower level.
- The clock does not simply follow how much TensorE has to do. With 96 matmuls a pair it was 1.00 twice (e9), with 80 in another order 1.00 twice (e1), with 80 in the changed kernel 0.76 to 0.94, with 64 it was 0.76 to 0.94 (e6) and, with no other work in the way, 1.00 in three stretches (e12; e13, the same with the blocks, in four). The kernel before had 0.80 to 0.90 in chunks that other work lengthened and 1.00 in those of 12.60. In these rows the low stretches are mostly those in which holds come on top of the regular pauses, but e1 and e9 have the holds too, and e3 ran at 1.00 where the changed kernel with the same gaps ahead fell to 0.50; what decides it no run here tells.
- The kernel with units one head ahead (e1) had executions of 1152.95 to 1162.43 at granted clocks of 0.933 down to 0.916, the shorter mostly at the higher clock. The kernel before had 1160.07 to 1163.45 at 0.915 to 0.922 on the same chip, with no such order. Whether the ring passes the clock on more, or only has more clock to pass on, is not told apart.
- VectorE steps of 128x16 took 1.96 and 1.93 behind GpSimd subtractions of 2.07 and 2.09, and 0.17 and 0.18 without them.
